# Edges to the node itself taken from the products instead of gathered, in a four-part graph network

## The reference

```python
edge_index = stack([src, dst])
x = layernorm(x + L0(x, edge_index))        # 4 layers: x = relu((x + sum_{dst} x[src]) @ W1 + b1) @ W2 + b2
x = layernorm(x + L1(x, edge_index, et8))   # relu(x @ root + bias + sum over 8 kinds of mean (x @ W[r])[src])
x = layernorm(x + L2(x, edge_index, et16))  # relu(sum alpha[k] * (x @ Wrel[k])[src] + indegree * (x @ update)), k = et16 of the edge
x = layernorm(x + L3(x, edge_index, et8))   # relu(sum (gate * (x @ W[k] + bias[k]))[src] + x @ loop), k = et8 of the edge
```

## Time and profile before

| | us |
|---|---|
| median of 3 runs | 2251.51 (2251.2 to 2252.34) |
| the profiled execution | 2252.56 |
| its span, first to last instruction | 2250.8 |
| ahead of the layers (adjacency is built) | 0 to 212 |
| four layers | 212 to 657 |
| gathers of pass one | 668.8 to 1188 |
| gathers of pass two | 1188 to 1712 |
| gathers of pass three | 1712 to 2238 |

### The profile page before, as it was taken

One profiled execution on the slowest core, in us unless ns is written; L12 is line 12 of the kernel. 1 busy time (PEld: TensorE's weight loads), 2 busy tenths in 40 slices (PEclk: granted clock), 3 DMA queues, 4 the chain that ended last, 5 costly groups with the idle time before them and its releaser, 6 DMA issues.

```text
span 2250.8 us, 31616 instructions
## 1 busy us (share of the span) xinstructions
PE 1463.2 (65%) x7538; PEld 989.7 (44%) x7539; DVE 906.3 (40%) x2269; ACT 599.7 (27%) x1689; POOL 1360.4 (60%) x1574
## 2 busy tenths in 40 slices
PE   4776999999987777777764655555455433434433
PEld 2332554545456665666653533343333333323333
DVE  7887122213673444444445533333344212212212
ACT  3776000000023333333331644444343000000000
POOL 5000166720007777777777777777777777777775
PEclk8888999999988989989897876667677756565565
DMA  1000011100213333333333222222222222222221
GB/s 31 0 0 10 15 9 12 11 3 0 59 54 109 94 113 112 95 112 110 95 113 97 72 81 79 71 80 79 71 81 84 56 56 56 55 56 56 55 56 46
DMA packets 126652, 137.49 MB, mean 61 GB/s; under 512 B 80706, under 2 KB 97866, under 8 KB 123433
## 3 DMA queue, kind: packets, MB, share of 16 engines
q0 software_dynamic: 40896, 81.94, 13.9%
q1 hardware_dynamic: 85673, 54.54, 8.1%
HBM read 91.88 MB, written 44.52 MB: 61 GB/s over the span
## 4 chain that ended last, share of the span: by engine, by line
POOL 50%; PE 21%; issue 18%; ACT 5%; DVE 2%; ACTq 1%; DMA 1%; POOLq 1%; SPq 0%; DVEq 0%
POOL adj L1013 49%; PE acc L1315 18%; ACT adj L1714 5%; PE misc L1251 1%; PE acc L1586 1%; PE acc L1202 1%; ACTq L1707 1%; DVE adj L2607 0%; DMA adj<-table,adj 0%; DVE adj L2606 0%; ACTq L1714 0%; POOLq L1009 0%; PE acc L1251 0%; ACT adj L1773 0%; PE acc L1204 0%
## 5 line engine op out<-in xcount | busy, mean ns | idle before, releaser
L1013 POOL DMA_INDIRECT adj<-table,adj x832 | 793.5, 954 | 253.6 <-issue 252.9
L1586 PE MATMUL acc<-adj 128*128 x1760 | 364.5, 385 | 499.7 <-DMA adj<-table,adj 253.3
L1586 PEld LDWEIGHTS acc<-adj 128*128 128x128 f32 x1760 | 328.5, 285 | 560.3 <-issue 560.2
L1013 POOL DMA_INDIRECT adj<-tablex,adj x416 | 392.8, 944 | 210.9 <-issue 126.5
L1773 ACT ACTIVATE adj<-adj 128x128 f32<-128x128 f32 x832 | 264.5, 390 | 581.0 <-DMA adj<-tablex,adj 315.2
L1315 PE MATMUL acc<-adj,feat 128*128 (+1 forms) x2100 | 406.8, 354 | 8.4 <-issue 8.4
L1513 PE MATMUL acc<-adj 128*128 128x128 f32 x1664 | 245.3, 310 | 124.1 <-ACT adj L1773 113.9
L1997 DVE TENSOR_TENSOR adj<-acc,drel 128x768 f32<-128x768 f32 (+1 forms) x148 | 139.9, 948 | 423.6 <-PE acc L1586 423.3
L1513 PEld LDWEIGHTS acc<-adj 128*128 128x128 f32 x1664 | 228.8, 220 | 167.2 <-issue 167.1
L1315 PEld LDWEIGHTS acc<-adj,feat 128*128 (+1 forms) x2100 | 186.2, 98 | 217.1 <-issue 13.1
L959 POOL TENSOR_TENSOR node_rep<-node_rep,compb 128x128 f32<-128x128 f32 x128 | 58.5, 457 | 272.4 <-DMA node_rep<-in_L_gnn_weight_dram 263.5
(11 more groups left out here) (352 smaller groups left out, 1297.6 us busy)
## 6 DMA issues: line engine op xcount, KB each, us to landing
table<-adj SPq DMA_DIRECT2D x24, 1024.0 KB, 4.1
adj<-table,adj POOLq DMA_INDIRECT x834, 2.5
table<-adj SPq DMA_DIRECT2D x25, 512.0 KB, 2.9
adj<-tablex,adj POOLq DMA_INDIRECT x416, 2.5
table<-adj SPq DMA_DIRECT2D x25, 64.0 KB, 2.0
out_dram<-adj SPq DMA_DIRECT2D x24, 64.0 KB, 1.5
temp<-in_x_dram SPq DMA_DIRECT2D x4, 256.0 KB, 3.1
wrel<-node_rep SPq DMA_DIRECT2D x16, 64.0 KB
```

The costliest lines, as they stand in the source:

```text
L1013: pool.indirect_dma_start(ring[:, p_, 0:D], None, rows_, bass.IndirectOffsetOnAxis(ap=gidx[:, p_:p_ + 1], axis=0)).then_inc(msgs_in[third_ ...
L1586: last = nc.tensor.matmul(acc[:, bass.ds(blk[s], width)], hot[:, c, j, :], ring_flat[:, bass.ds(place[s], width)], start=False, stop=True, ...
```

## The change

In passes two and three the edge of a node to itself is no longer gathered in 22 of the 25 turns (turns 2 to 23). Its row (node, kind) is among the products of the node's own block, so VectorE picks it there with a 0/1 mask over the kinds and adds it up: 16 operations a block in pass one (into loop_rows, added in pass two with the weight w2), 8 a block in pass two (into `rest`). One tile a turn, the eighth (EMPTY_AT = 7), is emptied for it: each edge of that tile moves to the place of a nearby edge to the node itself ("hole"), and the tile is neither gathered, weighted nor multiplied.

Where the holes are is found during the layers: POOL copies the destinations' beginnings to lists, finds for each of 22 x 128 nodes the last edge in three steps (by tile, by eighth of a tile, by edge; 22 gathers each), and scatters the codes, nodes and kinds of the moved edges to 11 small tables in DRAM; SP reads them back ahead of pass one, and VectorE puts them in place in turn 2 of pass one. The core of the diff:

```diff
-EARLY_SLICES = (range(0, 6), range(6, 11), range(11, 16), ())
+EARLY_SLICES = (range(0, 9), range(9, 13), range(13, 16), ())
 # SP, start
+            sp.dma_start(next1_i[0:EVENQ, :], ...)      # three loads of the destinations, shifted by one
             sp.dma_start(firsts_i, every_tile(0, TILES)).then_inc(ends_in, 16)
+            hold(sp, ends_in, ENDS_IN)
+            sp.dma_start(first_list, firsts_i).then_inc(ends_in, 16)
 # SP, behind the layers
-                sp.wait_ge(edges_out, SWAPPED * 16)
-                sp.dma_start(moved[:, :, :], edges0.rearrange("(t p) w -> p t w", p=P)).then_inc(edges_in, 16)
 # SP, ahead of pass one
+                sp.wait_ge(edges_out, (SWAPPED + 2 * LN) * 16)
+                sp.wait_ge(loops_in, (LISTED + 4 * LN) * 16)
+                sp.dma_start(moved[:, :, :], ...)
+                for g in range(KINDS_OF_LIST):          # 11 times three loads of the small tables
 # POOL, start
+            nc.gpsimd.tensor_tensor(next1_i[:, :], next1_i[:, :], ids_i[:, 0, :], ALU.subtract).then_inc(before_set, 1)
 # POOL, gathers
-                    for j in range(SIZES[c]):
+                    for j in range(SIZES[c] - (1 if c == 1 and emptied(ph, u) else 0)):
 # POOL, layers (in place of the slices and edges_part in turn)
+                slices(0, 4)
+                pool.wait_ge(late_counted, LISTS_SET)
+                for g in range(KINDS_OF_LIST):
+                    for list_, none in ((hole_codes[g], ...), (hole_nodes[g], no_hole)):
+                        pool.dma_start(by_place(list_), ...).then_inc(loops_in, 16)
+                pool.dma_start(edge_codes...[:, FROM_TILE:TILES], tile16[:, FROM_TILE:TILES]).then_inc(loops_in, 16)
+                pool.dma_start(eighths..., [[P // 16, (TILES - 1) * (P // 8)], [1, 1]]).then_inc(loops_in, 16)
+                for k, o in ((0, here_i), (1, behind_i)):
+                    pool.dma_start(o, [[1, P], [TPT * P, LN], [1, 1]]).then_inc(edges_in, 16)
+                pool.wait_ge(ends_in, ENDS_IN + 16)
+                pool.wait_ge(loops_in, LISTED * 16)
+                pool.dma_start(firsts_b, first_list.partition_broadcast(P)).then_inc(edges_in, 16)
+                slices(4, 9)
+                pool.wait_ge(late_counted, NODES_SET)
+                found_rows(lambda b: sixteen[:, b, :], lambda b: eighths, row_i)      # 22 indirect DMAs
+                slices(9, 13)
+                pool.wait_ge(late_counted, EIGHTS_SET)
+                found_rows(lambda b: eight[:, b, :], ...)                             # 22 indirect DMAs
+                slices(13, 16)
+                for n in range(SWAPPED // 4):
+                    edges_part(n)
+                pool.wait_ge(late_counted, HOLES_SET)
+                found_rows(lambda b: found[:, b:b + 1], lambda b: edge_codes, row_i)  # 22 indirect DMAs
+                for h in range(LISTS):                                                # 2 x 3 x 11 scatters
+                    if h > 0:
+                        pool.wait_ge(edges_out, (SWAPPED + 2 * h * KINDS_OF_LIST) * 16)
+                    for b, g in of_half:  pool.indirect_dma_start(hole_nodes[g], ...)
+                    pool.wait_ge(loops_in, (LISTED + 3 * LN + h * KINDS_OF_LIST) * 16)
+                    for b, g in of_half:  pool.indirect_dma_start(loop_codes[g], ...)
+                    for b, g in of_half:  pool.indirect_dma_start(hole_codes[g], ...)
                 passes(False)
 # VectorE, layers
+                    if l == 0 and not general:  code_lists()        # sets LISTS_SET
+                        loop_nodes()                                # l == 1, ahead of edge_places(): NODES_SET
+                    if l == 2 and not general:  loop_eighths()      # EIGHTS_SET
+                        if l == 2 and c == 4 and not general:
+                            loop_holes()                            # behind split_chunk of chunk 4: HOLES_SET
-                        edges_moved()                               # l == 3; now in turn 2 of pass one
 # VectorE, turn 2 of pass one
+                    if isinstance(t.k, int) and t.num() == LB:
+                        edges_moved()
+                        loops_taken()
 # VectorE, per block of pass one (a third each behind block_sum, ahead of and behind the one-hots)
+                for r in range(lo, hi):
+                        dve.wait_ge(picked, ...)
+                        ins = nc.vector.scalar_tensor_tensor(mine, rows_, of_r, mine, ALU.mult, ALU.add)
 # VectorE, per block of pass two
+                        for r in range(R3):
+                            nc.vector.scalar_tensor_tensor(own, stage[:, b.r, r * D:(r + 1) * D], own_kind3[...], own,
+                                                           ALU.mult, ALU.add).then_inc(picked, 1)
```

More of the change, by code:

```diff
@@ L409, in gnn @@
         zerob = sb("zerob", [P, KB], BF16)
+        hole = zerob[:, :].bitcast(F32)
+        here_i, behind_i, slot_c, slot_d, row_i, node_i, found = (hole[:, i * LN:(i + 1) * LN].bitcast(I32) for i in range(7))
+        here_f, node_f, tile_f, place_n, ends_f = (hole[:, i * LN:(i + 1) * LN] for i in (0, 7, 8, 9, 10))
+        more_f, many_f = (place_f[:, i * LN:(i + 1) * LN] for i in range(2))
+        loop_i = late[:, 2 * SWAPPED:2 * SWAPPED + LN].bitcast(I32)
+        assert 11 * LN <= KB // 2 and LN <= SWAPPED and 2 * LN <= 4 * 15
         epst = sb("epst", [P, 1])
@@ L1035, in released @@
                     for c in range(len(SIZES)):
[L1036 to L1037 removed]
+                        for i in range((r - ph + 1) % AHEAD_T, TURNS if c < 2 else TURNS - 1, AHEAD_T):
+                            pool.sem_inc(msgs_in[r][c], 16 * (SIZES[c] - (1 if c == 1 and emptied(ph, At(0, i)) else 0)))
             def table_written(ph, general):
@@ L1769, in take @@
                     return
-                hold(act, msgs_in[third_of(ph, u)][c], msgs_before(ph, u, c) + 16 * SIZES[c])
-                for j in range(SIZES[c]):
+                hold(act, msgs_in[third_of(ph, u)][c], msgs_upto(ph, u, c))
+                for j in range(SIZES[c] - (1 if c == 1 and emptied(ph, u) else 0)):
                     o = ring[:, place_of(ph, u, c) + j, 0:D]
@@ L2285, in layers @@
                 for l in range(LAYERS):
+                    if l == 0 and not general:
+                        code_lists()
                     if l == 1 and not general:
+                        loop_nodes()
                         edge_places()
+                    if l == 2 and not general:
+                        loop_eighths()
                     if l < LAYERS - 1:
@@ L2373, in body @@
                     if before.exists():
-                        table_parts(1, before)
+                        table_parts(1, before, now=False)
+                    own = before.exists() and picks(before)
                     if b.exists():
                         block_sum(1, t, b, False)
+                        if own:
+                            own_rows(before, 0, 4)
                         block_norm(1, b)
@@ L2459, in table_parts @@
                     nc.vector.tensor_copy(own, acc[:, SIDE_AT[1]:SIDE_AT[1] + D]).then_inc(prod_free[SIDE], 1)
+                    if not general and picks(b) and now:
+                        own_rows(b, 0, R2)
                 else:
```

323 lines of the change are left out of this document (276 added, 47 removed).

## The result

The changed kernel takes 2391.15 us (median of four runs, 2388.55 to 2393.69) against 2251.36 for the kernel before: a ratio of 1.062, 95% interval 1.0607 to 1.0634. That is 140 us more; forecast were 91, with a range up to 2395. The profiled execution has a span of 2391.6 us, 140.8 more than before.

What follows compares the result with a forecast made beforehand. POOL's gapless issue of gathers, 1.26 us each, and the time that queue starts were taken as the bound. Terms -55.4 + 5 + 126.4 + 6 + 9 = +91 us on 2252.6 gave 2343 us, range 2300 to 2395.

Steps and rivals of the forecast that it cites:

- What is taken away: Passes two and three: 44 gathers fewer at 1.26 us each on POOL, -55.4 us, all on the path.
- The in-order queue: Layers: new work on POOL ahead of passes() holds back the memset of near_i and edge weights; +126.4 us, layer 1's 27 included.
- Rival (1): New POOL work is hidden because one-word DMAs cost little besides 0.30 us of issue; 2227 us, or 2211 if altogether; chance 0.08.
- one wait for a landing, 2.5: In POOL's finds and scatters ahead of the memset of near_i: just one wait for a DMA landing, 2.5 us.
- Rival (2): Single words land slowly, 7.4 ns a piece, so layer 1 waits 133 us instead of 27; 2449 us; chance 0.10 above 2395.
- The first neighbour: SP loads layer 1's matrices behind nine slices that wait for POOL's lists; TensorE gets them 27 us late.
- just in time: POOL's own list ahead of the holes ends at 586, against loop_holes ending at 588.5 with layer 1 late.
- Set-up: Start of the kernel: added loads, a memset, and POOL and VectorE operations cost +5 us (4 to 7).
- Restarts at the lower clock: Two stalls of TensorE each cost a start at the lower clock, +6 us for both.
- Borders: Own-row picks on the path between passes: about 3 us into pass two, 6 into pass three, +9 us.
- The range: 2300 to 2395 us, chance 0.79; the top is for layer 1 late by 75 us.
- the signs named in advance: near_i memset at 690 to 710, first gather near 800, TensorE waits for matrices and carries, 394 + 394 gathers, pauses of 3 and 6.

Runs made afterwards that it cites:

- Experiment 6: Changed kernel without VectorE's sums of own rows (15 of 16 operations a block in pass one, all 8 in pass two); first gather to end 1530.5 us.
- experiment 1: Changed kernel with the passes' head (memsets of near_i, kinds_i and the pads) ahead of POOL's wait for the holes and its finds; 2303.09 us.
- experiment 3: Changed kernel with the loop_codes tables 16 times larger, so that words of neighbouring nodes stand 64 bytes apart; span 2351.5 us.
- experiment 4: Changed kernel with the copy of 6640 words into the list of eighths issued by SP at the start instead of by POOL in the layers; span 2353.5 us.
- experiment 5: Changed kernel with slices per layer as before the change (6, 5, 5 ahead of the loads of matrices); span 2369.6 us.
- experiment 7: Changed kernel with ScalarE's wait for POOL's last list of places moved behind the adjacency; span 2371.0 us.
- best3: The first of 9 to 12 plus the 22 fills and codes copy on SP's queue and the edit of experiment 8; 2229.66 us, ratio 0.990.
- best4: best3 with VectorE's loop_eighths behind chunk 4 of layer 1 and the memset of xn behind the first eleven scatters; 2233.03 us, ratio 0.990.
- best5: best4 with the memsets of near_i and kinds_i behind all 22 finds instead of the first six; 2208.55 us, ratio 0.981.
- experiment 2: Changed kernel with the scatters of loop_codes last in each half, changing places with those of hole_codes; span 2378.7 us.
- experiment 8: Changed kernel with the own-row sums of blocks 22 and 23 behind the copies of block 24; first gather to end 1534.9 us.
- the first of 9 to 12: Changed kernel with edits of experiments 2, 3, 4, 5, 7, loop_holes behind chunk 3, memsets behind the first six finds; 2233.49 us, ratio 0.992.

## Why the prediction was right, and where it was off

**What is taken away** held: 44 gathers fewer, and POOL without a wait for VectorE, TensorE or ScalarE inside the passes. The stretch from the first gather on is 38.8 us shorter instead of 46.4, since the gathers that are left take 4 to 9 ns more each: 6.9 us in all, which the sum did not have. Experiment 6 gives 2.8 of them to the sums of own rows; the 4 ns of passes two and three are no more than the spread between runs.

**The in-order queue** as the large term held, and experiment 1 shows it: with the memset moved, that memset comes 129 us sooner and carries_turned 141. The 88 indirect DMAs took 603.17 to 737.81 less the wait of 23.2, 111.4 us, for 110.9 forecast. Rival (1) is answered by the groups of POOL: a one-word scatter costs POOL 0.97 us.

**The step that failed is "one wait for a landing, 2.5".** That wait took 23.2 us, and the loads of near_i, for which I had taken no more than before (5.2 us from the memset to early_weights), took 20.5. Together 36 of the 50 us between forecast and measured, from one cause, the neighbouring words of loop_codes (experiment 3); some 7 of the 36 are the longer landings of this execution. The nearest row was the landing of gathers and of scatters with 16 bytes a row; no row of the kernel before has words scattered side by side in DRAM. Rival (2) had slow words in it, but put them into the list of eighths, and its price was for reading. (The eighths were slow too, at some 4.2 ns a word where the sum had at most 1.6 for the landing; next paragraph.)

**The first neighbour** came out at 27 forecast and 30.1 measured, with two terms wrong in it. The fills cost 0.72 us and not 1.26, the eighths 2.3 and not 5.8, the two lists 1.4 each and not 3.1: POOL was through with the first of them at 344.7, 20.5 us after slice 3, where I had 41 for all. Against that stood 28.9 us in which POOL could not go on with its next list, where I had 13 for the landing of the eighths; issued by SP that copy took 27.7 (experiment 4). That the lateness of layer 1 went whole into the sum was too simple: by experiments 5 and 6 about 6 of some 25 us counted by themselves, the rest was covered by POOL's own list, which I had called just in time.

**Set-up**: the +5 are what the runs show with a short last operation of POOL (224.9 less 219.8). The 5.8 above it are that operation drawn out beside VectorE's and ScalarE's wait for it (experiment 7).

**Restarts at the lower clock**: +6 forecast; the two stretches behind the stalls are 2.7 and 2.0 longer. TensorE stood from 643 to 777 in the second stall. Its granted clock is 0.50 in that time (the row of 673 to 696 us, last section), the lower level of 1.2 GHz, and the 24 products behind it took 7.2 us instead of 5.3, less than the 8.3 of the earlier trace rows:

```profile
777.69 7.22 PE L1447 MATMUL acc<-adj,feat 128*128 x24
```

**Borders**: 9 forecast, 9.9 measured, but the other way round, 6.3 into pass two and 3.6 into pass three. Into pass two the sums of two blocks lie ahead of the last copies, not of one; into pass three the last block's rows go out ahead of its sums.

**The range** held by luck. Its top, 2395, was left for layer 1 late by 75 us; layer 1 was 30 late, and what filled the room were the late landings, which the sum had at 2.5 and 5.2. Two of the signs named in advance show it: the memset of near_i came at 738 and not at 690 to 710, the first gather at 848 and not near 800. The other signs came as named: TensorE's waits ahead of turn_matrix(1) and for the carries, the counts of gathers, the two pauses.

## What to carry to other kernels

Work that "fits into idle time" of an engine also has a place in that engine's order: look at the first instruction behind it that somebody waits for, and move that ahead before anything is made faster. When a list of work becomes the bound, taking pieces out of it pays only until the next wait in it: best3 and best4 shortened what stands ahead of a memset that could not come before 576, and gained next to nothing; best5 moved work from behind that memset to ahead of it, and gained 1%. Words that are scattered one by one to DRAM should not be neighbours there. And before a difference between two traces is put down to an edit, look at how much the same stretch differs between runs in which it was not edited.

## What the runs showed of the hardware

A scatter of 128 one-word rows to neighbouring words in DRAM took some 4.3 us of the queue a table (experiment 2). DMAs issued behind such scatters landed late: those of hole_codes after 25.0 us (median) in the changed kernel and some 21 in experiments 6 to 8, and SP's loads of near_i reached VectorE 16 to 32 us after their memset instead of 5. With the words 64 bytes apart the scatters behind landed in 2.1 us. A busy share does not reveal it. This is the row of the changed kernel for most of POOL's wait of 23.2 us (stretch, its length, busy PE, PEld, DVE, ACT, POOL, each with its count, granted clock, DMA share, GB/s), with nothing moved and a DMA share of 0.00:

```profile
673.00:696.00 23.00, 0.00 (x0) 0.00 (x0) 0.00 (x0) 0.00 (x0) 0.00 (x0) 0.50 0.00 0
```

The Trainium skill, "DMA: Bandwidth & Descriptors", section "Specifications", says that below 512 bytes the DMA engines read, modify and write. The runs show a cost only for neighbours: words apart landed in 2.1 us, rows of 16 bytes in 2.3.

POOL stood 28.9 us (24 to 26 in the runs of experiments 1 to 3 and 5 to 8) between two direct DMAs with no wait written between them, behind one of 6640 words that takes 27.7 us to land when SP issues it. A direct DMA of 256 pieces cost POOL 0.72 us, one of 6640 words 2.3.

One and the same operation of POOL took 1.4 to 20.5 us beside a stream of VectorE's operations. In the changed kernel it ended when that stream paused (49.9 us after the start, POOL's end 50.6), but no pause is needed: in experiment 7 it ended after 2.9 us and in the first of 9 to 12 after 20.5 with the stream going on. Near its end VectorE's operations were longer than their like; in experiment 7 these four took 1.41 us, and 1.01 elsewhere in the stream:

```profile
44.07 1.41 DVE L2153 TENSOR_SCALAR feat<-temp,feat 128x300 bf16<-128x300 int16 x4
```

The Trainium skill, "SBUF — State Buffer", section "Who interferes with whom", says that the two share a pair of ports, and that where VectorE's operation needs that pair too, one of them holds it for a whole instruction while the other is blocked. The traces fit that, with the 0.4 us more on VectorE's side and the 1.4 to 20.5 us on POOL's; which of the two goes first, and why in one run so much later than in another, they don't show.
